# An adaLN block on one core: the second layernorm's statistics and normalisation go to VectorE

## The reference

```
h  = layernorm(x) * (1 + ca) + sa
q, k, v = split(h @ w_qkv + b_qkv)            # 8 heads of 64
attn = softmax(q^T k / 8)                     # 64 x 64 for each head, over the tokens
a  = (v attn) @ w_fc + b_fc + h
x2 = x + ga * (layernorm(a, eps 1e-6) * gamma + beta)
h2 = layernorm(x2, eps 1e-5) * (1 + cb) + sb
xr, xk = mixes of h2 with h2 of the token before (mu_r, mu_k)
out = x2 + gb * sigmoid(xr W_r) * (relu(xk W_k)^2 W_v)
```

## Time and profile before

| | |
|---|---|
| median of 3 runs | 819.67 us (819.04 to 819.78) |
| profiled execution, span from first to last instruction | 817.3 us |
| the median less this span | 2.4 us |
| PE / VectorE / ScalarE / GpSimd busy in it | 679.4 / 645.1 / 456.3 / 581.0 us |
| mean granted clock of PE | 0.934 |
| chain that ended last | GpSimd 46%, VectorE 21%, "issue" 17%, PE 10%, ScalarE 3% |

### The profile page before, as it was taken

One profiled execution on the slowest core, in us unless ns is written; L12 is line 12 of the kernel. 1 busy time (PEld: TensorE's weight loads), 2 busy tenths in 40 slices (PEclk: granted clock), 3 DMA queues, 4 the chain that ended last, 5 costly groups with the idle time before them and its releaser, 6 DMA issues.

```text
span 817.3 us, 12317 instructions
## 1 busy us (share of the span) xinstructions
PE 679.4 (83%) x3938; PEld 588.9 (72%) x3938; DVE 645.1 (79%) x1064; ACT 456.3 (56%) x935; POOL 581.0 (71%) x841
## 2 busy tenths in 40 slices
PE   4958786986989878998889969898789987898786
PEld 1847675875878766887768858787668876697675
DVE  4595978958988689886889589886898868858765
ACT  0324664564845467455655648464674557556754
POOL 5155998698766886778866987668867788618763
PEclk8989997999989999899989999899998999899789
DMA  9122021111211112010210111111120101000003
GB/s 312 48 72 72 1 85 52 33 40 53 59 53 45 51 58 77 26 45 26 83 51 32 38 51 58 51 45 51 58 77 26 46 0 32 26 26 27 26 1 103
DMA packets 40809, 43.22 MB, mean 53 GB/s; under 512 B 2696, under 2 KB 38832, under 8 KB 40784
## 3 DMA queue, kind: packets, MB, share of 16 engines
q1 hardware_dynamic: 38704, 40.24, 15.5%
q10 hardware_dynamic: 2080, 2.68, 1.0%
HBM read 26.06 MB, written 16.85 MB: 53 GB/s over the span
## 4 chain that ended last, share of the span: by engine, by line
POOL 46%; DVE 21%; issue 17%; PE 10%; ACT 3%; DMA 2%; POOLq 1%; DVEq 0%; ACTq 0%
POOL xk_lo L482 6%; POOL xb L464 5%; DVE x L912 4%; POOL y L487 4%; DVE wqkv_sb L935 4%; POOL ag L439 4%; POOL ag_a L439 3%; DVE t_buf L905 3%; POOL rs_o L456 2%; POOL ag L433 2%; POOL ag L427 2%; DVE t_buf L931 2%; DVE st L918 2%; POOL wv_aug L471 2%; POOL ag L429 2%
## 5 line engine op out<-in xcount | busy, mean ns | idle before, releaser
L1289 PE MATMUL att<-m_sb,z_t 128*128 128x256 f32 x496 | 112.8, 380 | 13.1 <-DVE t_buf L905 12.2
L905 DVE SCALAR_TENSOR_TENSOR t_buf<-att,rs_o,g_row 128x256 f32<-128x256 f32 x124 | 51.4, 477 | 83.0 <-POOL rs_o L456 82.9
L1173 PE MATMUL work<-wvf_lo,k_hi 128*128 128x256 f32 x248 | 80.7, 325 | 43.0 <-issue 36.4
L702 ACT ACTIVATE z<-x,ag 128x256 f32<-128x256 f32 x128 | 66.4, 590 | 81.7 <-POOL ag L449 81.7
L1289 PEld LDWEIGHTS att<-m_sb,z_t 128*128 128x128 f32 x496 | 92.3, 190 | 27.0 <-issue 15.1
L1173 PEld LDWEIGHTS work<-wvf_lo,k_hi 128*128 128x128 f32 x248 | 54.4, 219 | 53.8 <-issue 44.6
L464 POOL TENSOR_TENSOR xb<-x_in,rows 128x1024 f32<-128x1024 f32 x32 | 79.4, 2488 | 16.0 <-DMA rows<-row_scratch 8.5
L1271 PE MATMUL gram<-z 128*128 128x256 f32 (+1 forms) x512 | 89.1, 327 | 0.0
L1271 PEld LDWEIGHTS gram<-z 128*128 128x128 f32 x512 | 79.8, 191 | 6.6
L482 POOL TENSOR_TENSOR xk_lo<-wqkv_sb,xk_hi 128x1024 fp32r<-128x1024 f32 x30 | 75.6, 2521 | 8.8 <-ACT xk_hi L665 8.8
L1173 PE MATMUL work<-xk_lo,w_rk_hi 128*128 128x512 f32 x122 | 54.1, 444 | 32.8 <-POOL xk_lo L482 32.8
(11 more groups left out here) (194 smaller groups left out, 2028.8 us busy)
## 6 DMA issues: line engine op xcount, KB each, us to landing
x_in<-in_L_attn_x_dram SPq DMA_DIRECT2D x32, 512.0 KB, 3.5
out_dram<-y SPq DMA_DIRECT2D x29, 512.0 KB, 3.0
rows<-row_scratch SPq DMA_DIRECT2D x16, 128.0 KB, 3.3
rows<-row_scratch SPq DMA_DIRECT2D x8, 256.0 KB, 3.1
wqkv_sb<-in_L_attn_w_qkv_dram ACTq DMA_DIRECT2D x1, 1536.0 KB, 12.9
x<-in_L_wmod_dram SPq DMA_DIRECT2D x1, 1024.0 KB, 14.8
out_dram<-x_in SPq DMA_DIRECT2D x2, 512.0 KB, 2.9
x<-in_L_wmod_dram SPq DMA_DIRECT2D x1, 512.0 KB, 4.7
```

The lines of the kernel that those rows point to most:

```text
L702: ins = nc.scalar.activation(z2[:, t], x2[:, j, t], ACT.Identity, bias=ag_2[:, s, 1, t:t + 1], scale=ag_2[:, s, 7, t:t + 1])
L905: ins = nc.vector.scalar_tensor_tensor(t_buf[:, t], att_banks(j, alone)[t // 2][:, (t % 2) * D:(t % 2 + 1) * D], rs_o[:, s, t:t + 1], g_ro ...
L1173: mm(dst, s_hi, m_lo, start=start, stop=False)
L1289: ins = mm(att_banks(j, alone)[q][:, (t % 2) * D:(t % 2 + 1) * D], z_t[:, j, k, t * P:(t + 1) * P], m_sb[:, k], start=(k == 0), stop=(k == ...
```

## The change

The constants: minus_one goes, eps_ln (1e-5) comes. The tile ag_2 goes, small tiles mv_2, md_2, q_2, mean_2, var_2, ve_2 and rs_2 come. stats_2 on VectorE gets five small instructions behind its four bn_stats, GpSimd's rstd_2 shrinks to two, and make_z2 moves from ScalarE to VectorE as tensor_scalar (subtract mean, multiply by rstd). prep_qk is cut in its two halves in rows 1 to 6, with make_z2(b, 0) and low_k(b - 1, 3) between.

```
@@ GpSimd
             def rstd_2(b, j):
-                i, ag = CH * b + j, ag_2[:, j % 2]
-                layernorm_factors(i, st_2[:, j % 2], ag, st_2_done, ag_2_step, rs_2_step, EPS_LN)
-                nc.gpsimd.tensor_tensor(ag[:, 0], ag[:, 3], minus_one[:], ALU.mult).then_inc(rs_2_step, 1)
-                pool.wait_ge(rs_2_step, 2 * i + 2)
-                nc.gpsimd.tensor_tensor(ag[:, 1], ag[:, 0], ag[:, 7], ALU.mult).then_inc(rs_2_ready, 1)
+                i, s = CH * b + j, j % 2
+                pool.wait_ge(mv_2_done, i + 1)
+                nc.gpsimd.tensor_tensor(ve_2[:, s], var_2[:, s], eps_ln[:], ALU.add).then_inc(ve_2_done, 1)
+                pool.wait_ge(ve_2_done, i + 1)
+                nc.gpsimd.tensor_tensor(rs_2[:, s], ve_2[:, s], neg_half[:], ALU.pow).then_inc(rs_2_ready, 1)
@@ ScalarE: make_z2 and its calls go
-            def make_z2(b, j):
-                i, s = CH * b + j, j % 2
-                act.wait_ge(rs_2_ready, i + 1)
-                for t in range(NT):
-                    ins = nc.scalar.activation(z2[:, t], x2[:, j, t], ACT.Identity, bias=ag_2[:, s, 1, t:t + 1],
-                                               scale=ag_2[:, s, 7, t:t + 1])
-                ins.then_inc(z2_ready, 1)
@@ VectorE, stats_2
                 ins.then_inc(st_2_done, 1)
+                dve.wait_ge(st_2_done, i + 1)
+                nc.vector.tensor_tensor(mv_2[:, s], st_2[:, s, :, 1:3], st_2[:, s, :, 4:6], ALU.add)
+                nc.vector.tensor_tensor(md_2[:, s], st_2[:, s, :, 1], st_2[:, s, :, 4], ALU.subtract).then_inc(mv_2_step, 1)
+                dve.wait_ge(mv_2_step, 2 * i + 1)
+                nc.vector.scalar_tensor_tensor(q_2[:, s], md_2[:, s], 0.25, md_2[:, s], ALU.mult, ALU.mult).then_inc(mv_2_step, 1)
+                nc.vector.tensor_scalar(mean_2[:, s], mv_2[:, s, :, 0], 0.5, None, ALU.mult)
+                dve.wait_ge(mv_2_step, 2 * i + 2)
+                nc.vector.scalar_tensor_tensor(var_2[:, s], mv_2[:, s, :, 1], 1.0 / D, q_2[:, s], ALU.mult, ALU.add).then_inc(mv_2_done, 1)
+
+            def make_z2(b, j):
+
+                i, s = CH * b + j, j % 2
+                dve.wait_ge(rs_2_ready, i + 1)
+                wait_past(dve, z2_turned, 2 * i)
+                for t in range(NT):
+                    ins = nc.vector.tensor_scalar(z2[:, t], x2[:, j, t], mean_2[:, s, t:t + 1], rs_2[:, s, t:t + 1],
+                                                  ALU.subtract, ALU.mult)
+                ins.then_inc(z2_ready, 1)
@@ VectorE, row_steps
                 else:
-                    prep_qk(n)
+                    prep_qk(n, (0,))
+                    make_z2(b, 0)
                     low_k(b - 1, 3)
+                    prep_qk(n, (1,))
                     make_z(n, 2)
                     make_x2(b, 1)
                     stats_2(b, 1)
                 mix(b, 0)
                 low_xr(b, 0)
+                make_z2(b, 1)
...
                 low_k(b, 0)
                 make_z(n, 3)
+                make_z2(b, 2)
                 mix(b, 1)
...
                 low_xr(b, 2)
+                make_z2(b, 3)
                 gate_o(b, 1)
```

More of the change, by code:

```diff
@@ L87, in adaln_block @@
         last_c = sb("last_c", [P, D])
-        neg_half, half, quarter, minus_one, eps_att = (
-            sb(n, [P, NT]) for n in ("neg_half", "half", "quarter", "minus_one", "eps_att"))
+        neg_half, half, quarter, eps_ln, eps_att = (
+            sb(n, [P, NT]) for n in ("neg_half", "half", "quarter", "eps_ln", "eps_att"))
         wqkv_sb = sb("wqkv_sb", [P, KD, 3 * HD])
@@ L143, in adaln_block @@
         st_2 = sb("st_2", [P, 2, NT, 6])
-        ag_2 = sb("ag_2", [P, 2, 8, NT])
+        mv_2 = sb("mv_2", [P, 2, NT, 2])
+        md_2, q_2, mean_2, var_2, ve_2 = (sb(n, [P, 2, NT]) for n in ("md_2", "q_2", "mean_2", "var_2", "ve_2"))
+        rs_2 = sb("rs_2", [P, 2, NT])
         z2 = sb("z2", [P, NT, D])
@@ L257, in adaln_block @@
         st_2_done = sem("st_2_done")
-        ag_2_step = sem("ag_2_step")
-        rs_2_step = sem("rs_2_step")
+        mv_2_step = sem("mv_2_step")
+        mv_2_done = sem("mv_2_done")
+        ve_2_done = sem("ve_2_done")
         rs_2_ready = sem("rs_2_ready")
@@ L413, in build_constants @@
                 nc.gpsimd.memset(half[:], 0.5).then_inc(const_ready, 1)
-                nc.gpsimd.memset(minus_one[:], -1.0).then_inc(const_ready, 1)
+                nc.gpsimd.memset(eps_ln[:], EPS_LN).then_inc(const_ready, 1)
                 nc.gpsimd.memset(quarter[:], 0.25).then_inc(const_ready, 1)
@@ L714, in row_steps @@
                     copy_z_t(n, 1)
-                    make_z2(b, 0)
                 else:
@@ L727, in row_steps @@
                 take_r(b, 0)
-                make_z2(b, 1)
                 take_k(b, 0)
@@ L731, in row_steps @@
                 squares(b, 3)
-                make_z2(b, 2)
                 copy_z_t(n, 3)
@@ L743, in row_steps @@
                 split_xk(b, 2)
-                make_z2(b, 3)
                 exps(n)
@@ L990, in prep_now, with prep_qk @@
                 nc.vector.tensor_copy(d_now[:], mod_col[:, 2:4, b]).then_inc(prep_step, 1)
-            def prep_qk(b):
+            def prep_qk(b, ks=(0, 1)):
                 dve.wait_ge(prep_base, b + 1)
-                for k in range(KD):
+                for k in ks:
                     n = P if k < KD - 1 else P - 1
@@ L1000, in prep_qk @@
                                                          ALU.mult, ALU.add)
-                ins.then_inc(qk_ready, 1)
+                if ks[-1] == KD - 1:
+                    ins.then_inc(qk_ready, 1)
             def split_rk():
```

## The result

The changed kernel takes 874.86 us, the median of 4 runs (873.59 to 875.11), against 819.36 (818.29 to 819.78) for the kernel before on the same chip: ratio 1.067, 95% interval 1.0648 to 1.0693. It is 55.5 us slower. The forecast was 881.0.

The account below looks back on a forecast made before the run. No engine was full; the order of waits decided, with VectorE and GpSimd blocking each other. Stages summed to +10.3 us a row, taken as 9.4: six rows 56, row 0 +5, last row 0, so +61, 881 us; range 828 to 903.

Parts of the forecast that it names:

- The mechanism: Loop rows: VectorE instructions with SBUF tensors wait out large GpSimd ones (blocking, 12.8 us a row before); new work meets more.
- stage 5: Last of five parts of a loop row, cut at each make_x2 and the softmax: rs_a earlier, 0.6 idle goes, -0.6 us.
- the last row: Last row: VectorE ends z2(2) at 767.1, ScalarE 770.2, but low_k behind z2(0) makes mix(0) 4.8 later: 0.
- Stage 1: First part of a loop row: z2(0) and others meet prep_wv, rstd_o and xb; 21.3 against 17.5 us, +3.8.
- Stage 2: Second part of a loop row: xb, xk_lo(0), y block VectorE, the 3.5 us rs_o wait is filled; +3.5 us.
- Stage 3: Third part of a loop row: 2.15 us new work that nothing hides, one xb as before; +1.8 us.
- Stage 4: Fourth part of a loop row: new work, blocks by y, xb and xk_lo(2), waits for PE filled; +1.8 us.
- Row 0: First row: fewer large GpSimd instructions and more waits to take the work in; +5 us.
- (a): Rival: new work fits into VectorE's idle time, -2.2 us a row, 804 us; chance 0.10.
- (b): Rival: the change does nothing, as (a) with some 2.2 us a row of blocking, 820 us; chance 0.03.
- (c): Rival: blocking only at today's rate, 56% of large GpSimd time, +1.2 us a row, 832 us; chance 0.17.
- (d): Rival: PE falls behind as well, longer holes put another 2 to 3 us on a row, 905 us; chance 0.06.

Follow-up runs that it names:

- e6_low_k_first: The changed kernel with low_k(b-1, 3) in front of make_z2(b, 0), and in the last row stats_2(b, 1) and low_k in front; 859.56 us.
- e5_forms: Not the reference's computation: forms of VectorE instructions measured alone and beside three 1024-column GpSimd additions; 121.48 us.
- e9_after_pow: The changed kernel, GpSimd's large instructions cut to 2 or 4 columns per group from row 1, two 4-column powers before each; 739.54 us.
- e8_before_pow: The kernel before, GpSimd's large instructions cut to 2 or 4 columns per group from row 1, two 4-column powers before each; 762.21 us.
- e2_stats_only: The kernel before with only the second layernorm's small statistics moved to VectorE, z2 staying on ScalarE; 797.78 us, ratio 0.9764.
- e1_z2_only: The kernel before with only the z2 pass moved to VectorE, statistics staying on GpSimd; 889.66 us, ratio 1.0867.
- e7_both_stats: The kernel before with the small statistics of both the second and first layernorm moved to VectorE, z2 on ScalarE; 807.03 us, ratio 0.9859.
- e4_after_narrow: The changed kernel with GpSimd's large instructions made on 2 or 4 columns of each group from row 1 on; 735.85 us.

## Why the prediction was right

**The mechanism** held in the first four stages of the loop rows; in stage 5 and in the last row it did not come as told. Per row it said: 8.6 us of new work, blocking from 12.8 to 26 us, VectorE's idle time filled. Measured in row 4: new work 7.8, blocking 12.8 to 23.6, idle time 16.4 to 5.9. The blocking, in the order of the timeline: mv 0.65, x2 0.5, z2(0) 3.7, prep_qk 2.15; xr mix 2.0, z2(1) 2.1, wvf_hi 2.1; make_z 2.1; x2 1.9, difference 2.2, z2(3) 2.1; make_z 2.1. Own work and blocking give 7.8 + 10.8 = 18.6 against the 18.3 by which busy time rose.

**Stage 1**, predicted +3.8, came out at +2.4. The walk is found again link by link: rs_2 idle 1.0 (0.91), prep_wv's first half under z2(0), its second half under the next tile, xb on the second half of prep_qk. Only rstd_o, which was to block the last tiles for 0.4, did not (0.40 us a tile at its side). z2(0) lost 3.7 instead of 4.6, and stats_2's small instructions lost 0.65 to y, with 0.5 on x2, where the walk had 0.6 and 0.8.

**Stage 2**, +3.5 predicted, +2.65 measured: xb under the mix, xk_lo(0) under z2(1) and y on W_v's scaling came as told (the last on the cast wvf_hi, not on wvf_lo); the small ones were not blocked. **Stage 3** +1.8, measured +1.4; z2(2) unblocked as assumed. **Stage 4** +1.8, measured +1.6, with the three blocks of the walk: x2, the difference, and xk_lo(2) on z2(3). **Stage 5** -0.6, measured -0.1: here the step failed. The wait for rs_a was to go; it is still there, 0.58 us as before. GpSimd's nine instructions for it begin behind the bn_stats that end at 564.45 and are done at 567.83, and the change does not touch them:

```profile
567.87 3.41 DVE L881 TENSOR_SCALAR z<-x_in,ag_a 128x255 f32<-128x255 f32 x4 [0.58 <-POOL ag_a L442]
```

**The sizes.** The six rows cost 47.9 us where the sum had 56. Two terms were a little large: the small instructions measure 0.65 us a chunk (506.07 to 506.73), not 0.8, and the blocking per row was 2.4 us less than walked; the sum had already taken off some 1 us for that. Row 0 was +5, measured +5.8 (92.7 to 98.5). The set-up in front of it, taken as unchanged, is 1.8 shorter. **The last row** was the term that failed in its reasoning: it was put at 0, and it costs 4.2 us (81.4 to 85.6). Its cause was named, low_k(b-1, 3) behind the waiting z2(0), so that mix(0) comes later; but the walk let VectorE's shorter z2 pass win that back. Counted from the row's first make_x2, mix(0) starts 6.4 us later (22.3 instead of 16.0), not 4.8, and z2(2), which was to end 3 us earlier than ScalarE's, ends 5 us later. The timeline of VectorE in that row, before:

```profile
751.84 1.23 DVE L931 TENSOR_TENSOR t_buf<-h2t 128x1024 f32<-128x1024 f32 x1 [0.20 <-DVE x L912]
```

and after:

```profile
794.75 3.15 DVE L898 TENSOR_TENSOR x<-t_buf,xb 128x1024 f32<-128x1024 f32 x1
...
810.06 1.23 DVE L935 TENSOR_TENSOR t_buf<-h2t 128x1024 f32<-128x1024 f32 x1 [4.85 <-ACT h2t L654]
```

y blocks x2(1), and then VectorE waits 4.85 us for h2. e6_low_k_first puts 2.2 of the 4.2 us down to that order; where the other 2 come from was not tried. The errors of the terms are 47.9 - 56 = -8.1, +0.8, +4.2 and -1.8: -4.9 in all, of the 6.1 between 881.0 and 874.86. Most of the rest is the 2.4 us between span and median, which are 1.6 here, and rounding.

**A reading that was wrong.** The prediction had the blocked wvf_lo, x2 and difference end 1.2 to 1.4 us behind the end of the GpSimd instruction under them. By the trace of before it is 0.55, 1.08 and 1.08 us (wvf_lo to 485.28, xb to 484.73; x2 to 509.20, y to 508.12; the difference to 512.81, xb to 511.73): somewhat less than each takes by itself, 0.69 and 1.22. The sum is made of the time that each loses, and does not use this figure.

**z2's price.** The row of the first layernorm's z, 1.36 us for four, decided, and that was right: 1.37 when free. The single tiles (shortest, median, longest ns):

```profile
L921 DVE TENSOR_SCALAR z<-x,mean,rs x128: 399/403/2492, 78.0 to 841.4; 128x256 f32<-128x256 f32 x128
```

The Trainium skill, page VectorE: DVE Perf Modes, section "Mode 2×_2P — use both read ports for one tensor", with the same page's errata table, gave an estimated 0.8 us for four. The runs differ from it (403 ns a tile here, 408 alone in e5_forms, some 1.37 us for four), and the measurement decides.

**What is blocked.** The Trainium skill, GPSIMD Engine Reference, section 1, names two-input instructions and those in 2-port mode as the ones that contend with GpSimd. The runs agree: z2's form and the cast wvf_hi with one input, and the additions with two, were blocked in e5_forms or in the row above; bn_stats and the form that reads PSUM were not. That z2's form runs in a 2-port mode is not shown: it takes 403 ns for 256 columns, where the cast takes 427 ns for 512 when nothing blocks it (in the kernel before), and both are blocked.

**The rivals.** (a), the new work fits into idle time, needed blocking to rise by less than 2.2 us a row, and (b) by about 2.2; it rose by 10.8. e9_after_pow beside e8_before_pow goes the way of (a), by 22.7 us, where GpSimd's large instructions are out of SBUF. (c), blocking at today's rate of 56%, would be 18.3 us of 32.6; it is 23.6, 72%. (d), PE falls behind as well, is there in small: PE's granted clock is 0.83 in stage 1, where it was 1.00, but stage 4 went the other way, 0.83 to 0.92, and over the six loop rows it is 0.93 against 0.95. How much of the loss PE's share is was not separated: the new order of e6_low_k_first has a clock of 1.00 in stage 1, but the 1.3 us that this stage wins are the 0.91 us of VectorE's wait and 0.4 us less of busy time.

**The signs.** As told: the row at about 105 us (103.4), rs_o's wait under 4 us a row (2.5), VectorE over 85% (89%), z2's mean well over 0.39 (0.80) and longest 2.49, the means of make_z's tiles (499 to 629 ns) and of L997, now L1001 (1539 to 2072), up, ScalarE at 392, GpSimd down by 101 us. Wrong: the mean of the xk mixes fell, 1027 to 851 ns, and that of the xr mixes rose, 774 to 885. In the row above the instruction of GpSimd falls on the pair in front (508.47), where in the earlier trace rows it fell on the pair behind (498.58).

## What to carry to other kernels

Before moving work from one of VectorE and GpSimd to the other, lay their two timelines side by side and mark which instructions have their tensors in SBUF: what counts is not the busy time that moves but what each new instruction meets, and it meets most where a semaphore of one engine releases the other just as the first goes on to something large. A short chain of small instructions on GpSimd was worth moving (e2_stats_only, 0.976 of the time, interval 0.972 to 0.981), a pass over whole tiles was not (e1_z2_only, 1.087), and moving a second short chain, when most of VectorE's waits were gone, gave back 8 to 9 us. An instruction that waits for another engine should not stand in front of one that is ready to run: exchanging the two was worth about 14 us.

## What the runs showed of the hardware that was not expected

- The size of the VectorE instruction does not matter to how long it is blocked: an addition on 4 columns, 155 ns by itself, took up to 2319 ns beside a 2342 ns instruction of GpSimd (e5_forms), and 2.38 us in e7_both_stats. The forecast had that such instructions can be blocked, but costed them mostly free.
- The blocking is mutual: GpSimd's own 2342 ns addition took up to 3375 ns beside VectorE's, and its 0.2 us addition of epsilon took 1.18 us at 488.08 in the changed kernel.
- A power on 4 columns keeps GpSimd busy for 1 us and did not block: with two of them for each narrowed instruction z2's tiles had a mean of 439 ns (e9_after_pow), against 441 without them (e4_after_narrow) and 800 in the changed kernel.
